# Cross attention with a routed expert layer: the last pair of batches taken out of the loop

## The chip, the cores and the metric

The program runs on one core of one Trainium2 chip. Its time is the device time of one execution in microseconds (us). A core has TensorE (PE in the rows, with its weight loads listed apart as PEld), VectorE (DVE), ScalarE (ACT), GpSimd (POOL) and SyncE (SP), which here only issues DMAs. Each runs its own instruction stream in order, and they meet at semaphores.

## The reference

```python
x = x + xattn(layernorm(x), ctx_768, Wq, Wk, Wv, Wo, bo)
x = x + ffn(layernorm(x), router_weight, router_bias, gate_w, up_w, down_w, shared_*)

# xattn: 16 heads of 64, x (16, 256, 128), context (16, 1601, 96)
sim  = einsum('bhid,bhjd->bhij', q, k) * SCALE
out  = einsum('bhij,bhjd->bhid', softmax(sim), v)   # then @ Wo + bo

# ffn: 32 experts of width 64, four per token, and a shared expert of width 128
scores = sigmoid(tokens @ router_weight.T)          # two of four groups, then the best four
hidden = silu(tokens @ gate_w) * (tokens @ up_w)    # per expert
y      = sum of topk_w * (hidden @ down_w) + shared expert
```

## The kernel before

**Attention.** The 16 batches are taken in pairs by a hardware loop `Fori(0, B // 2)`, whose body holds both batches (`par` 0 and 1). A batch is four groups of four heads (`i` 0 to 3), so there are 64 groups. I number them from 0: the last batch is groups 60 to 63. A group has S = 13 steps over tiles of 128 keys (the last of 65). In a step `t`, PE makes the scores of tile `t` (`scores`, six matmuls of 512 columns: the precision is kept by splitting every operand in a hi and a lo part, hi\*hi + hi\*lo + lo\*hi), and adds tile `t-2` to the output (`weigh`, six more). ACT makes the exponentials twice (`exp`: `p_full`, then the rounded `p_hi`), and the difference `p_lo` is made by DVE, or in steps 3, 5, 7 and 9 by POOL (`POOL_STEPS`). `p_full` has two buffers, so `exp(s)` waits for `p_lo` of `s-2`. At the end of a group PE makes the scores of tiles 0 and 1 of the next group.

**Side jobs.** Between these, PE does small jobs into the two PSUM banks of `side`, in the places that `PLACES` and `EXTRA` give: M (32 per group, the scores by which the next group's maximum is found; DVE reduces each), T (the maxima turned to a row, which a DMA sends into `qT_hi`), Q (two per group, the queries of the group after next), Y (four per group, the output projection of the four heads before, which DVE adds to `x1` in `add_head`), and once per batch L and N (normalised tokens turned, for the next batch and for the expert layer) and R (router logits). `s_fill` counts the jobs made, `s_drain` those used, and PE waits for the job before the last one to be drained. POOL splits the next batch's context into hi and lo, one quarter per group (`piece_hi`, `piece_lo`). The loop is the same for every batch, so the last batch also makes L, Q, M, T, two scores and the split for a batch that does not exist.

**Between the stages.** After the loop PE projects the last four heads (`project_head`), turns the last batch's tokens, makes their logits and turns the first routing weights, each of these behind the DVE work that feeds it (`add_head` four times, `token_stats`, `normalise`, `keep_x2f`). ACT and DVE split the first NA = 5 of the expert weights (`weights_hi`, `weights_lo`) there. The other twelve land by DMA after the loop and are split between the first pairs.

**Expert stage.** Straight code: eight chunks `c` of 512 tokens, in each NP = 17 pairs `q` of experts (pair 0 is the shared one). `g` = 17c + q counts all pairs. For a pair PE makes gate and up (`three` twice, three matmuls each), spreads the routing weights over the rows (`rep`, one matmul, not for pair 0), and projects the hidden values of pair g-3 down (three matmuls). ACT does Silu and `h_hi`, DVE `gu_mul` and `hid`, POOL `h_lo`. PE's gate of pair g waits for Silu of g-2 and its up for `hid` of g-2. `turn_routing(c+1)` stands after pair 10 of chunk c, and `keep_routing` on ACT keeps it in `wT`.

## Time and profile before

| | us |
|---|---|
| three runs | 3332.54, 3332.04, 3326.1 (median 3332.04) |
| the profiled execution | 3330.03 |
| its span in the trace | 3327.9 |
| PE busy | 3285.5 (99%) |
| DVE busy | 2399.7 (72%) |
| ACT busy | 1937.8 (58%) |
| POOL busy | 1062.4 (32%) |

Attention fills the span from about 38 to 2986.7 us, the expert stage that from 2997.6 us to the end. A matmul's row gives a duration that overlaps with the next one's (they are pipelined), so what an instruction costs PE is the distance from its start to the next start. Idle time in front of an instruction, with what ended it, stands in square brackets.

### The profile page before, as it was taken

Reading aid. Unit: us, or ns where it says so; the run is one execution under the profiler, and the core shown is the slowest. Engines: PE = TensorE matmul, PEld = TensorE weight load, DVE = VectorE, ACT = ScalarE, POOL = GpSimd, SP = SyncE. Lnnn points to the kernel's source line nnn. Section 1 sums busy time; section 2 is a strip of 40 time slices with the busy share of each in tenths; the row PEclk is TensorE's granted clock in tenths of the full one; section 3 lists DMA queues with packets and bytes.
Section 4 is the critical chain, followed back from the end, with each engine's and each line's share of the span. In section 5 each row is a group of like instructions: output and inputs, shape, how many; then the busy total and the mean of one; then the engine's idle time right before and its main releaser. Section 6 shows DMA issues by size and latency. Waiting matters only on the chain.

```text
span 3327.9 us, 50432 instructions
## 1 busy us (share of the span) xinstructions
PE 3285.5 (99%) x15589; PEld 2616.2 (79%) x15589; DVE 2399.7 (72%) x4954; ACT 1937.8 (58%) x2239; POOL 1062.4 (32%) x724
## 2 busy tenths in 40 slices
PE   8999999999999999999999999999999999999999
PEld 6777777777787777777777777777777777777887
DVE  6777777777777777777777777777777777777655
ACT  4655556665566555565555565555656566655554
POOL 4322233222332222322223322233222332225555
PEclk9999999999999999999999999999999999999999
DMA  2000000000000000000000000000000000010000
GB/s 91 1 16 1 17 1 16 1 1 17 1 16 1 17 1 16 1 9 10 1 16 1 17 1 16 1 16 2 1 16 1 17 1 16 1 45 4 7 7 10
DMA packets 8682, 35.98 MB, mean 11 GB/s; under 512 B 1657, under 2 KB 2306, under 8 KB 8130
## 3 DMA queue, kind: packets, MB, share of 16 engines
q1 hardware_dynamic: 8386, 32.29, 3.1%
q8 instruction: 154, 2.52, 0.3%
q14 instruction: 142, 1.16, 0.1%
HBM read 29.92 MB, written 2.10 MB: 10 GB/s over the span
## 4 chain that ended last, share of the span: by engine, by line
issue 71%; POOL 18%; PE 9%; DVE 1%; POOLq 0%; ACT 0%; DVEq 0%; ACTq 0%
POOL p_lo L391 12%; POOL cT_lo L380 2%; PE st L629 2%; POOL v_lo L382 2%; PE st L631 2%; PE st L630 2%; POOL cT_hi L372 1%; POOL v_hi L373 1%; PE op L629 1%; PE op L631 1%; PE op L630 1%; PE side L676 1%; POOL rstd L309 1%; DVE gu_mul L1123 0%; POOLq L390 0%
## 5 line engine op out<-in xcount | busy, mean ns | idle before, releaser
L760 ACT ACTIVATE p_full<-st 128x1024 f32<-128x1024 f32 (+1 forms) x832 | 855.9, 1029 | 1158.4 <-PE st L520 1154.1
L1032 DVE TENSOR_REDUCE m_part<-side 128x1 f32<-128x402 f32 x2048 | 1095.0, 571 | 544.0 <-PE side L460 544.0
L391 POOL TENSOR_TENSOR p_lo<-p_full,p_hi 128x1024 fp32r<-128x1024 f32 x256 | 649.9, 2539 | 2087.6 <-ACT p_hi L763 2087.6
L763 ACT ACTIVATE p_hi<-st 128x1024 fp32r<-128x1024 f32 (+1 forms) x832 | 850.9, 1023 | 0.0
L1020 DVE TENSOR_TENSOR p_lo<-p_full,p_hi 128x1024 fp32r<-128x1024 f32 (+1 forms) x576 | 700.5, 1216 | 140.2 <-ACT p_hi L763 116.7
L460 PE MATMUL side<-cT_hi,qT_hi 96*128 96x402 f32 x2048 | 563.0, 346 | 0.0
L514 PE MATMUL st<-qT_hi,cT_hi 97*128 97x512 f32 (+1 forms) x1668 | 539.8, 405 | 2.3 <-DMA qT_hi<-m_row 2.3
L528 PE MATMUL op<-p_hi,v_hi 128*97 128x512 f32 (+1 forms) x1664 | 527.7, 398 | 6.1 <-DVE p_lo L1020 6.1
L517 PE MATMUL st<-qT_lo,cT_hi 96*128 96x512 f32 (+1 forms) x1668 | 528.0, 397 | 0.0
L520 PE MATMUL st<-qT_hi,cT_lo 96*128 96x512 f32 (+1 forms) x1668 | 523.2, 395 | 0.0
L531 PE MATMUL op<-p_lo,v_hi 128*97 128x512 f32 (+1 forms) x1664 | 519.4, 393 | 0.0
L534 PE MATMUL op<-p_hi,v_lo 128*97 128x512 f32 (+1 forms) x1664 | 519.2, 393 | 0.0
L460 PEld LDWEIGHTS side<-cT_hi,qT_hi 96*128 96x128 f32 x2048 | 385.1, 188 | 114.0
L520 PEld LDWEIGHTS st<-qT_hi,cT_lo 96*128 96x128 f32 (+1 forms) x1668 | 307.0, 184 | 83.7
L517 PEld LDWEIGHTS st<-qT_lo,cT_hi 96*128 96x128 f32 (+1 forms) x1668 | 308.9, 185 | 80.9
L531 PEld LDWEIGHTS op<-p_lo,v_hi 128*97 128x97 f32 (+1 forms) x1664 | 269.9, 162 | 115.6
L534 PEld LDWEIGHTS op<-p_hi,v_lo 128*97 128x97 f32 (+1 forms) x1664 | 269.8, 162 | 114.8
L514 PEld LDWEIGHTS st<-qT_hi,cT_hi 97*128 97x128 f32 (+1 forms) x1668 | 297.7, 186 | 31.6 <-issue 2.8
L528 PEld LDWEIGHTS op<-p_hi,v_hi 128*97 128x97 f32 (+1 forms) x1664 | 265.1, 163 | 38.0 <-DVE p_lo L1020 8.4
L414 POOL TENSOR_TENSOR h_lo<-hid,h_hi 128x512 fp32r<-128x512 f32 x136 | 175.8, 1293 | 142.7 <-ACT h_hi L826 142.6
L912 DVE SCALAR_TENSOR_TENSOR x<-side,recip,x 128x128 f32 (+1 forms) x520 | 158.6, 347 | 11.2 <-DVE recip L909 2.6
L1123 DVE TENSOR_TENSOR gu_mul<-st,act_g 128x512 f32<-128x512 f32 x128 | 88.4, 691 | 102.7 <-PE side L676 95.7
(153 smaller groups left out, 2629.5 us busy)
## 6 DMA issues: line engine op xcount, KB each, us to landing
keys_nat<-in_ctx_keys SPq DMA_DIRECT2D x18, 624.0 KB, 5.7
keys_tur<-in_ctx_turned SPq DMA_DIRECT2D x18, 603.0 KB, 4.9
out_x<-x SPq DMA_DIRECT2D x8, 256.0 KB, 2.0
x<-in_x SPq DMA_DIRECT2D x1, 1920.0 KB, 12.2
w_rest<-in_moe_w SPq DMA_DIRECT2D x1, 1152.0 KB, 7.4
qT_hi<-m_row SPq DMA_DIRECT2D x65, 4.0 KB
w_first<-in_moe_w SPq DMA_DIRECT2D x1, 960.0 KB, 4.7
aw<-in_attn_w SPq DMA_DIRECT2D x2, 448.0 KB, 5.3
```

The source lines that it names most:

```text
L391: pool.tensor_tensor(p_lo[:, slot(s), :], p_full[:, s % 2, :], p_hi[:, slot(s), :].bitcast(F32), ALU.subtract).then_inc(s_lo_pool, 1)
L460: return pe.matmul(where[:, 0:MAXW], qT_hi[0:DC, slot, tile * P:(tile + 1) * P], cT_hi[0:DC, par, part * MAXW:(part + 1) * MAXW], start=Tr ...
L514: pe.matmul(st[0:m, s % 2, j, :], cT_hi[:, par, keys], qT_hi[:, slot, halves[j]], start=True, stop=False)
L517: pe.matmul(st[0:m, s % 2, j, :], cT_hi[0:DC, par, keys], qT_lo[:, slot, halves[j]], start=False, stop=False)
L520: mm = pe.matmul(st[0:m, s % 2, j, :], cT_lo[:, par, keys], qT_hi[0:DC, slot, halves[j]], start=False, stop=True)
L528: pe.matmul(op[0:OW, j, :], v_hi[0:m, par, s, :], p_hi[0:m, slot(s), halves[j]], start=(s == 0), stop=False)
L531: pe.matmul(op[0:OW, j, :], v_hi[0:m, par, s, :], p_lo[0:m, slot(s), halves[j]], start=False, stop=False)
L534: mm = pe.matmul(op[0:OW, j, :], v_lo[0:m, par, s, :], p_hi[0:m, slot(s), halves[j]], start=False, stop=(s == S - 1))
L760: act.activation(p_full[0:m, s % 2, :], both(st[0:m, s % 2]), ACT.Exp, scale=SCALE)
L763: act.activation(p_hi[0:m, slot(s), :], both(st[0:m, s % 2]), ACT.Exp, scale=SCALE).then_inc(s_ex, 1)
L1020: dve.tensor_tensor(p_lo[0:m, slot(s), :], p_full[0:m, s % 2, :], p_hi[0:m, slot(s), :].bitcast(F32), ALU.subtract).then_inc(s_lo, 1)
L1032: dve.tensor_reduce(m_part[:, at:at + 1], where[:, 0:MAXW], AX.X, ALU.max).then_inc(s_drain, 1)
```

## The change

1. The loop runs over seven pairs of batches. The eighth pair is written out behind it with constants in place of registers (`turns`, `here`), its second batch with `last` set.
2. With `last`, nothing is made for what does not come: no L and Q in group 62, no M, T and Q in group 63, no scores of a next group, and no context is loaded or split in the last batch.
3. The expert weights land in one tensor `gud_raw` that lies over context and query buffers of batch 14 (each of these tensors is now two, one per half). Three DMAs are issued in group 60 and a small one in group 63. ACT splits weights 0 to 8 in group 62 and 9 to 16 in group 63, one behind an `exp`. DVE makes `gud_lo` in group 63, two behind a step, in place over `gud_raw`. The tokens of chunk 0 are split there too (`x2_hi_of(0)`, `x2_rest(0)`), and `wT` is cleared at the start of the program.
4. The expert stage begins right behind the last `weigh`. `turn_routing(0)` stands behind pair 0. The last batch's four heads are projected behind pairs 1 to 4, its tokens turned behind pair 9, its logits made behind pair 11, all in bank 1 of `op`. ACT changes its table to Exp and back behind pair 12. In every chunk `turn_routing(c+1)` moves from behind pair 10 to behind pair 14, `keep_routing` from 11 to 15.

```diff
-        def jobs_of(par, i):
-            return JOBS0 + par * PER_BATCH + offset[i]
+        def places(i, last=False):
+            drop = {2: "LQ", 3: "MTQ"}.get(i, "") if last else ""
...
+        def turns(eng, body):
+            with eng.Fori(0, B // 2 - 1) as bb:
+                for par in range(2):
+                    for i in range(NGB):
+                        body(bb, par, i, False)
+            for par in range(2):
+                for i in range(NGB):
+                    body(B // 2 - 1, par, i, par == 1)
...
+                if last and i == 0:
+                    sp.wait_ge(s_v, NG)
+                    sp.wait_ge(s_oe, NG - 3)
+                    load_moe_weights(0, 0, 4)
+                    load_moe_weights(1, 4, 10)
+                    load_moe_weights(2, 10, 16)
...
 # PE, end of a group
                 pv(S - 2)
+                if last and i == NGB - 1:
+                    pv(S - 1)
+                    return
...
-            pe.wait_ge(s_oe, NG + 1)
-            for h in range(GH):
-                pe.wait_ge(s_drain, JOBS_END + h - 1)
-                project_head(bank(JOBS_END + h), (NGB - 1) * GH + h, h * NQ)
-            pe.wait_ge(s_drain, JOBS_END + GH - 1)
-            turn_tokens(bank(JOBS_END + GH), B + 2, 2)
-            pe.wait_ge(s_drain, JOBS_END + GH + 1)
-            route_logits(bank(JOBS_END + GH + 1))
...
+            def last_batch_jobs(q):
+                where = op[:, 1, :]
+                if 1 <= q <= GH:
+                    h = q - 1
+                    pe.wait_ge(s_wk, 1)
+                    pe.wait_ge(s_drain, JOBS_END + h)
+                    project_head(where, (NGB - 1) * GH + h, h * NQ)
+                elif q == 9:
+                    pe.wait_ge(s_drain, JOBS_END + GH)
+                    turn_tokens(where, B + 2, 2)
+                elif q == 11:
+                    pe.wait_ge(s_drain, JOBS_END + GH + 1)
+                    route_logits(where)
...
+                    if g == 0:
+                        pe.wait_ge(s_rw, B)
+                        pe.wait_ge(s_oe, NG + 1)
+                        turn_routing(0)
                     if g >= 3:
                         down(g - 3)
+                    if c == 0:
+                        last_batch_jobs(q)
...
-                    if q == 10 and c + 1 < NCH:
+                    if q == 14 and c + 1 < NCH:
...
 # ACT, in a group
                     exp(s)
+                    if last and i == 2 and 1 <= s <= 9:
+                        weights_hi(s - 1)
+                    elif last and i == 3 and 2 <= s <= 9:
+                        weights_hi(s + 7)
+                    elif last and i == 3 and s == 1:
+                        x2_hi_of(0)
...
 # ACT, expert stage
+                    if g == 0:
+                        keep_routing(0)
+                    if g == 10:
+                        act.wait_ge(s_fill, JOBS_END + GH + 1)
+                        keep_x2(op[:, 1, :], slice(B * NQ, (B + 1) * NQ))
+                    if g == 12:
+                        act.preload_act_table(ACT.Exp)
+                        keep_exponentials(op[:, 1, :], JOBS_END + GH + 2)
+                        act.preload_act_table(ACT.Silu)
...
 # DVE, in a group
                     side_jobs(at[t][1])
+                    if last and i == NGB - 1:
+                        for q in (2 * t - 4, 2 * t - 3):
+                            if q < NP:
+                                weights_lo(q)
...
 # DVE, expert stage
+                    if c == 0:
+                        if 1 <= q <= GH:
+                            dve.wait_ge(s_drain, JOBS_END + q - 1)
+                            add_head(op[:, 1, :], JOBS_END + q, NG * GH + q, (T, T + 1))
+                        elif q == 5:
+                            dve.wait_ge(s_drain, JOBS_END + GH)
+                            token_stats((T, T + 1), 2)
+                        elif q == 7:
+                            normalise((T, T + 1), 2, B + 2)
+                        elif q == 10:
+                            keep_x2f(op[:, 1, :], B + 1)
+                        elif q == 13:
+                            exponentials_seen(B + 1)
```

PE before, from the last `weigh` but one of group 63 to the first pair. L514 to L520 are the scores of a group that does not come, L540 the four heads, L427 and L432 tokens and logits, L635 `turn_routing(0)`, L629 to L631 `three`:

```order
L514 MATMUL st<-qT_hi,cT_hi 128x512 x2
L517 MATMUL st<-qT_lo,cT_hi 128x512 x2
L520 MATMUL st<-qT_hi,cT_lo 128x512 x2
L612 REGISTER_ALU
L612 COMPARE_AND_BRANCH
L540 MATMUL side<-B_all,oT 128x129 x8
L427 MATMUL side<-ident,xn 128x128 x2
L432 MATMUL side<-rwT,x2f 128x32 x2
L635 MATMUL op<-ident,w_all 64x128 x4
L629 MATMUL st<-x2_hi,gud_hi 128x512
```

PE now, from the last `weigh` (L549 to L555) through pair 0 (L642 to L644 twice); L648 is `turn_routing(0)`:

```order
L549 MATMUL op<-p_hi,v_hi1 97x512 x2
L552 MATMUL op<-p_lo,v_hi1 97x512 x2
L555 MATMUL op<-p_hi,v_lo1 97x512 x2
L642 MATMUL st<-x2_hi,gud_hi 128x512
L643 MATMUL st<-x2_lo,gud_hi 128x512
L644 MATMUL st<-x2_hi,gud_lo 128x512
L642 MATMUL st<-x2_hi,gud_hi 128x512
L643 MATMUL st<-x2_lo,gud_hi 128x512
L644 MATMUL st<-x2_hi,gud_lo 128x512
L648 MATMUL op<-ident,w_all 64x128 x4
```

The two scores are gone, pair 0 stands directly behind the attention, and the jobs that stood between the stages have moved behind the first pairs.

DVE before, in group 63. L1020 is `p_lo`, L1032 the reduction of one M, L1030 and L1019 the sums for its waits on registers, L909 and L912 `add_head`:

```order
L909 RECIPROCAL recip<-side 128x2
L910 REGISTER_ALU
L912 SCALAR_TENSOR_TENSOR x1<-side,recip,x1 128x128 x2
L1030 REGISTER_ALU
L1032 TENSOR_REDUCE m_part<-side 128x1
L1030 REGISTER_ALU
L1032 TENSOR_REDUCE m_part<-side 128x1
L1019 REGISTER_ALU
L1020 TENSOR_TENSOR p_lo<-p_full,p_hi 128x1024
```

DVE now, in the same steps. L1055 is `p_lo`, L1036 `weights_lo`, L948 the mark that the exponentials of R are seen, L936 and L939 `add_head`:

```order
L1055 TENSOR_TENSOR p_lo<-p_full,p_hi 128x1024
L1036 TENSOR_TENSOR gud_lo<-gud_raw,gud_hi 128x384 x4
L1055 TENSOR_TENSOR p_lo<-p_full,p_hi 128x1024
L948 MEMSET spare 128x1
L1036 TENSOR_TENSOR gud_lo<-gud_raw,gud_hi 128x384 x4
L1055 TENSOR_TENSOR p_lo<-p_full,p_hi 128x1024
L1036 TENSOR_TENSOR gud_lo<-gud_raw,gud_hi 128x384 x2
L936 RECIPROCAL recip<-side 128x2
L939 SCALAR_TENSOR_TENSOR x1<-side,recip,x1 128x128 x2
```

Where the 32 reductions of M stood, 17 splits of weights stand.

## Rows read from the trace of the kernel before

**Rows 1.** The page: busy time, share of the span and instructions by engine.
```profile
PE 3285.5 (99%) x15589; PEld 2616.2 (79%) x15589; DVE 2399.7 (72%) x4954; ACT 1937.8 (58%) x2239; POOL 1062.4 (32%) x724
```

**Rows 2.** Windows at the expert stage: window, its length, busy by engine, granted clock.
```profile
2997.50:3001.50 4.00, 4.00 (x11) 3.19 (x10) 0.69 (x1) 2.32 (x3) 0.00 (x0) 0.50 0.00 0
3001.50:3041.00 39.50, 39.50 (x176) 32.32 (x175) 29.81 (x46) 26.30 (x50) 23.80 (x19) 1.00 0.00 1
```

**Rows 3.** Timeline, PE, group 63 (start, us, engine, line, operation, count).
```profile
2959.72 0.53 PE L460 MATMUL side<-cT_hi,qT_hi 96*128 96x402 f32 x2
2960.08 0.63 PE L528 MATMUL op<-p_hi,v_hi 128*97 128x512 f32 x2
...
2979.69 0.28 PE L453 MATMUL side<-x_hi,A_hi 128*96 128x256 f32 x1
...
2981.11 0.63 PE L528 MATMUL op<-p_hi,v_hi 128*97 128x512 f32 x2
...
2982.50 0.62 PE L514 MATMUL st<-qT_hi,cT_hi 97*128 97x512 f32 x2
...
2983.90 0.62 PE L528 MATMUL op<-p_hi,v_hi 65*97 65x512 f32 x2
...
2986.69 1.06 PE L540 MATMUL side<-B_all,oT 97*128 97x129 f32 x8
```

**Rows 4.** Timeline, PE, from the stage change to the third pair.
```profile
2993.76 0.66 PE L427 MATMUL side<-ident,xn 128*128 128x128 f32 x2 [3.92 <-DVE xn L879]
...
2997.57 0.78 PE L629 MATMUL st<-x_hi,gud_hi 128*128 128x512 f32 x1
...
3002.46 0.40 PE L629 MATMUL st<-x_hi,gud_hi 128*128 128x512 f32 x1
```

**Rows 5.** Page: the exponentials, p_lo on DVE and on POOL (mean ns of one).
```profile
L760 ACT ACTIVATE p_full<-st 128x1024 f32<-128x1024 f32 (+1 forms) x832 | 855.9, 1029 | 1158.4 <-PE st L520 1154.1
L391 POOL TENSOR_TENSOR p_lo<-p_full,p_hi 128x1024 fp32r<-128x1024 f32 x256 | 649.9, 2539 | 2087.6 <-ACT p_hi L763 2087.6
L1020 DVE TENSOR_TENSOR p_lo<-p_full,p_hi 128x1024 fp32r<-128x1024 f32 (+1 forms) x576 | 700.5, 1216 | 140.2 <-ACT p_hi L763 116.7
```

**Rows 6.** Timeline, ACT, around the stage change.
```profile
2985.49 1.03 ACT L745 ACTIVATE oT<-op 97x1024 f32<-97x1024 f32 x1 [3.59 <-PE op L534]
...
2987.43 2.16 ACT L799 ACTIVATE gud_hi<-w_first 128x384 fp32r<-128x384 f32 x5
...
2997.34 1.28 ACT L819 ACT_TABLE_LOAD   x1
2998.64 0.59 ACT L810 ACTIVATE wT<-op 64x512 fp32r<-64x512 f32 x1
2999.23 0.60 ACT L844 ACTIVATE act_g<-st 128x512 f32<-128x512 f32 x1
```

**Rows 7.** Timeline, DVE: two heads added, one pair of experts, one weight split.
```profile
2988.26 0.17 DVE L909 RECIPROCAL recip<-side 128x2 f32<-128x2 f32 x1
...
2989.11 0.17 DVE L909 RECIPROCAL recip<-side 128x2 f32<-128x2 f32 x1
...
3004.34 0.69 DVE L1123 TENSOR_TENSOR gu_mul<-st,act_g 128x512 f32<-128x512 f32 x1 [0.20 <-PE side L676]
...
3005.67 0.93 DVE L1095 TENSOR_TENSOR gud_lo<-w_rest,gud_hi 128x384 fp32r<-128x384 f32 x1
```

**Rows 8.** Timeline, POOL, at that weight split.
```profile
3004.89 1.30 POOL L414 TENSOR_TENSOR h_lo<-hid,h_hi 128x512 fp32r<-128x512 f32 x1 [0.66 <-ACT h_hi L826]
```

**Rows 9.** Timeline, PE, a head projected in a running group.
```profile
2965.19 0.61 PE L540 MATMUL side<-B_all,oT 97*128 97x129 f32 x4
2965.55 0.72 PE L514 MATMUL st<-qT_hi,cT_hi 97*128 97x512 f32 x2
```

**Rows 10.** Waits (us in total, times, longest): PE and DVE where the loop jumps back.
```profile
PE op L528 <- DVE p_lo L1020: 6.1, 7, 1.0
DVE p_lo L1020 <- issue: 23.5, 7, 3.5
```

More of the change, by code:

```diff
@@ L139, in xattn_moe @@
         s_rl = sem("router_landed")
-        s_mw = sem("first_moe_weights_landed")
-        s_mr = [sem(f"other_moe_weights_{part}_landed") for part in range(3)]
+        s_mw = [sem(f"moe_weights_{part}_landed") for part in range(4)]
         s_id = sem("identity_ready")
@@ L407, in x2_rest, with body @@
                                    x2_hi[:, c % 2, :].bitcast(F32), ALU.subtract).then_inc(s_xxl, 1)
-            x2_rest(0)
+            def body(bb, par, i, last):
+                g = group_of(par, i)
+                for s in POOL_STEPS:
+                    pool.wait_ge(s_ex, bb * (2 * NGB * S) + (g * S + s + 1))
+                    pool.tensor_tensor(p_lo[:, slot(s), :], p_full[:, s % 2, :],
+                                       p_hi[:, slot(s), :].bitcast(F32), ALU.subtract).then_inc(s_lo_pool, 1)
+                    if s == 3 and i == 1:
+                        deviations(bb * 2 + (par + 2), slice(0, 4))
+                    elif s == 5 and not last:
+                        piece_hi(bb, par, i)
+                    elif s == 7 and not last:
+                        piece_lo(bb, par, i)
+                    elif s == 7 and i == NGB - 1:
+                        x2_rest(0)
+            turns(pool, body)
             for c in range(NCH):
@@ L459, in max_scores @@
                 tile, part = k % (NM // 4), k // (NM // 4)
-                return pe.matmul(where[:, 0:MAXW], qT_hi[0:DC, slot, tile * P:(tile + 1) * P],
-                                 cT_hi[0:DC, par, part * MAXW:(part + 1) * MAXW], start=True, stop=True)
+                return pe.matmul(where[:, 0:MAXW], qT_hi[slot][0:DC, tile * P:(tile + 1) * P],
+                                 cT_hi[par][0:DC, part * MAXW:(part + 1) * MAXW], start=True, stop=True)
             def turn_maxima(where):
@@ L587, in pv @@
                     weigh(s, par)
-                at = places(i)
+                at = places(i, last)
                 for t in range(2, S):
@@ L810, in keep_routing @@
                 act.activation(wT[0:2 * E, c % 2, :], op[0:2 * E, 1, :], ACT.Copy).then_inc(s_wk, 1)
-            after_attention(act)
-            x2_hi_of(0)
-            for q in range(NA):
-                weights_hi(q)
-            act.wait_ge(s_fill, JOBS_END + GH + 1)
-            keep_x2(bank(JOBS_END + GH), slice(B * NQ, (B + 1) * NQ))
-            keep_exponentials(bank(JOBS_END + GH + 1), JOBS_END + GH + 2)
-            act.preload_act_table(ACT.Silu)
-            keep_routing(0)
             def hidden_hi(g):
@@ L834, in _ @@
                     g = c * NP + q
-                    if c == 0 and NA <= q + 2 < NP:
-                        weights_hi(q + 2)
                     if q == 3 and c:
@@ L1005, in _, with weights_lo, body @@
             head_steps, loop_steps = steps[0], [0]
-            def body(bb, par, i):
-                g = group_of(par, i)
-                n = dve.snap(bb * (2 * NGB * S) + g * S)
-                jobs0 = jobs_of(par, i)
-                jobs = dve.snap(bb * (2 * PER_BATCH) + jobs0)
-                links = dve.snap(bb * links_per_turn)
+            def weights_lo(q):
+                dve.wait_ge(s_wh, q + 1)
+                dve.tensor_tensor(gud_lo[:, q, :, :], gud_raw[:, q, :, :],
+                                  gud_hi[:, q, :, :].bitcast(F32), ALU.subtract).then_inc(s_wl, 1)
+            def body(bb, par, i, last):
+                if par == 0 and i == 0:
+                    steps[0] = head_steps
+                g = group_of(par, i)
+                n = here(dve, bb * (2 * NGB * S) + g * S)
+                first_bank = jobs_of(par, i, last)
+                jobs = here(dve, bb * (2 * PER_BATCH) + first_bank)
+                place = job_at(i, last)
+                links = here(dve, bb * links_per_turn)
                 made = dict.fromkeys(KINDS, 0)
-                into = [dve.snap(bb * 4 + (2 * par + (i + (NGB - 1)) // NGB * 2 + q)) for q in range(2)]
+                into = [here(dve, bb * 4 + (2 * par + (i + (NGB - 1)) // NGB * 2 + q)) for q in range(2)]
                 def lo(s):
@@ L1025, in side_jobs @@
                         k = made[kind]
-                        j = job_at[i][kind][k]
+                        j = place[kind][k]
                         made[kind] += 1
-                        where, filled = bank(jobs0 + j), jobs + (j + 1)
+                        where, filled = bank(first_bank + j), jobs + (j + 1)
                         if kind == "M":
@@ L1064, in after_jobs @@
                         route_scores(links)
-                at = places(i)
+                at = places(i, last)
                 lo(0)
```

247 lines of the change are left out of this document (100 added, 147 removed).

## The prediction

> **What bounds the kernel.** I read the page first: PE is busy for 99% of the span, the next engine for 72% [rows 1]. So what counts is PE's work and the few places where it stands. The waits list them: seven of 0.9 us where the loop jumps back [rows 10], and the stage change, seen in the timeline and the windows. In group 63 PE works without a hole on things that nobody will use [rows 3]. Then it stands for up to 3.92 us behind the chain of DVE and ACT work that feeds its small jobs [rows 4], and when the pairs start, the granted clock is 0.50, the 1.2 GHz level, for 4.0 us [rows 2]. After that it is 1.00 and PE is busy all 39.5 us of the window [rows 2]. All sums are made against the profiled execution, 3330.03 us, 2.1 us more than its span. The three runs of before have their mean at 3330.2 and their median at 3332.04, so I take its time as typical.
>
> **Work that goes.** Two M cost PE 2960.08 - 2959.72 = 0.36 us, so 32 cost 5.8. The two Q of group 63 cost 2981.11 - 2979.69 = 1.42, and group 62's two as much, together 2.84. The two scores cost 2983.90 - 2982.50 = 1.40 each, together 2.80 [all rows 3]. L and T are three small matmuls; by 0.09 each and 0.09 for the slower start behind them (the duration 0.72 against 0.63) I take 0.4 [rows 9, 3]. Sum: 11.8 us, all on PE's path, as PE has no hole there.
>
> **What is late next in group 63.** Without M a step is two sets of six matmuls, 2 x 1.40 = 2.8 us of PE. ACT needs two exponentials of 0.92 to 1.03 [rows 5] and one `weights_hi` of 2.16/5 = 0.43 [rows 6], at most 2.5: it keeps up. POOL's `p_lo` takes 2.54 [rows 5], and from the end of a scores set to its `weigh` PE has four sets, 5.6 us, against 2.0 (exp) + 2.54 + some 0.2 of handing over. DVE's load in the whole group: nine `p_lo` of 1.22 are 11.0 [rows 5], 17 splits of about 0.41 are 7.0, four heads of 2989.11 - 2988.26 = 0.85 are 3.4 [rows 7], 21.4 in about 36 us (PE's 24 sets of 1.40, and 2.3 for the heads and R). The split's 0.41 is read so: the row shows 0.93, but POOL's `h_lo` ran until 3004.89 + 1.30 = 3006.19, 0.52 after the split's start, and 0.93 - 0.52 = 0.41 [rows 7, 8].
> That row also shows that a split does not run beside a POOL operation. The Trainium skill says so in SBUF — State Buffer, "Who interferes with whom": DVE and GpSimd share a port pair under an exclusive lock, and a DVE `tensor_tensor` with both inputs in SBUF contends with GpSimd's reads. It speaks against this change, since the M reductions that ran beside POOL's `p_lo` read PSUM and the 17 splits read SBUF; the trace agrees, with the 0.93.
> So I let each split wait for POOL's `p_lo`. In steps 3 to 10 that moves DVE's next `p_lo` to 1 to 2 us before PE needs it, which costs nothing. At the end the cover is gone: the last scores used to be followed by Q (1.42) and the next scores (1.40). Now it is last scores, two `weigh`, last `weigh`: 2.8 us, against exp 2.0 + `p_lo` 1.22 + 0.1, and the `p_lo` before it stands behind three heads. PE waits for 0.1 + 0.4 = 0.5. Bounds: 0, if DVE's queue is early, and 2.5, if a whole POOL `p_lo` lies in the way once.
>
> **The stage change.** Before, from 2986.69 (the end of the attention) to 3002.46 (gate of pair 2) are 15.8 us [rows 3, 4]. After, I call P the end of the last `weigh`. ACT keeps `oT` from P + 0.2 to P + 1.1, loads the table in 1.30 (2998.64 - 2997.34), makes Silu of pair 0 in 0.55 and `wT` in 0.59 (with the distance 2999.23 - 2998.64), and is through at P + 3.5 [rows 6]. PE meanwhile makes pair 0 (six matmuls at 0.23, from 39.50/176, 1.4 us), `turn_routing(0)` (four small ones, 0.45 as a head), gate and up of pair 1, stands at P + 3.2 until P + 3.6 for `wT`, and is at gate 2 at P + 3.8 without the head of pair 1. So 15.8 becomes 3.8: 12.0 us saved. This includes the half clock's share: the thirteen matmuls of pairs 0 and 1 took 3002.46 - 2997.57 = 4.9 us [rows 4], where thirteen at 0.23 take 3.0, so 1.9 us.
>
> **What comes back between the pairs.** Four heads, each 2965.55 - 2965.19 = 0.36 and 0.09 behind it [rows 9]: 1.8. Tokens (two small matmuls) 0.25, logits (two in the order, four in the trace) 0.45. The second head waits for the first `add_head`: Silu of pair 1 ends at P + 4.1, `gu_mul` and `hid` take 3005.67 - 3004.34 = 1.33 with their gap [rows 7], the head 0.85, which is P + 6.4, where PE arrives at P + 5.8: 0.6 us. From pair 3 DVE needs 1.33 + 0.85 = 2.2 us a pair and PE ten matmuls and a head, 2.3 + 0.45, so no more waits. The splits of twelve weights have left ACT and DVE there; token statistics, `normalise` and `keep_x2f` (about 1 us each) stand one to a pair. Sum: 3.1 us, bounds 2.5 (no wait) and 5 (each of four heads waits 0.6).
> The two table loads behind pair 12 cost ACT 2 x 1.30 + 0.3 = 2.9 us. Silu of pair 13 may start 2.3 us after its gate; it starts 1.8 after it. So nothing on PE, with 0.5 to spare.
>
> **Loop.** Six jumps back for seven. DVE stands 23.5/7 = 3.4 us at each, PE 6.1/7 = 0.9 [rows 10]. Saved 0.9. Behind the last jump PE went on at once: the heads begin where the scores end, 2986.69 [rows 3], so leaving the loop is free. `turn_routing` four pairs later, `wT` cleared on POOL at the start, and weights loaded two groups (about 90 us) ahead: 0, hidden by PE's matmuls, and if that cover went each of the first two would cost under 1 us, the small job that it is, and the third the weights' own split of 0.4 to 0.9 once. The waits that routing of the last batch brings in chunk 1 stay as they are.
>
> **Sum.** -11.8 + 0.5 - 12.0 + 3.1 - 0.9 = -21.1. 3330.0 - 21.1 = **3309 us**.
>
> **Rivals.**
> - **The lock holds DVE in group 63.** For it: the 0.93 [rows 7]. Each of POOL's four `p_lo` would push a DVE `p_lo` past PE's need by about 1 us and the end by 2: 4 to 6 us, so 3314. Against: the group has 36 - 21.4 = 14.6 us of DVE to spare, and four times 2.54 are 10.2. Chance 0.12.
> - **The clock falls again.** PE stands 0.4 and 0.6 us and waits at the end of group 63. For it: the 0.50 behind the old change [rows 2]. Against: 0.9 us at each jump back with the page's clock full. Price as before, 1.9 us, up to 4: 3311 to 3313. Chance 0.08.
> - **A table load costs ACT twice its row.** By rows: 1.3 us more in the seam, and 5.5 in place of 2.9 behind pair 12, which is 2.1 past what is to spare: 3312.4. Against it stands the row, where the next operation begins 1.30 after the load [rows 6]. Chance 0.03. The Trainium skill has this as its price: ScalarE: Activation LUTs, "What ACT_TABLE_LOAD costs", about 1283 ns and a drain of about 1380 ns for every switch. The trace agrees with the first part and shows no second.
> - **Slower: the straight pair is fetched too late.** If each of the eight written-out groups started with the 3.4 us that DVE stands at a jump [rows 10] and nothing hid it, 27 us would be added: 3336. It decides from 2.6 us a group. Against: the expert stage is straight code and PE stands nowhere in 39.5 us [rows 2]. Chance 0.02.
> The forecast has the remaining 0.75; a gain of 1 to 3 us beyond it (steps of group 63 that DVE's old drains slowed) is in its own range, 3304 to 3313.
>
> **Range and chances.** The runs of before span 6.4 us, which I add in part: 3302 to 3317. What a measurement can tell from no change is about 0.2%, 6.7 us. Every case but the last is faster by more than 13 us, so faster 0.95. Same 0.03, for a mix of losses that I have not seen, slower 0.02.
>
> **What would show it.** Group 63 about 36 us long in place of 46 (36 + 5.8 + 1.4 + 2.8), PE's waits in it under 1 us. The first Silu load at P + 1.1, `wT` at P + 3, the first matmul of the pairs at the end of the last `weigh`, clock 1.00 throughout. In chunk 0 one wait of PE, for the first `add_head`. Wrong would be: PE waiting on `p_lo` of steps 4 to 10 in group 63, more than 1 us on `hid` in pairs 13 to 15, or a hole at the starts of groups 56 to 62.

## The result, and the profile after

The changed kernel takes 3308.0 us (median of 3304.41, 3308.09, 3309.41 and 3307.89), the kernel before, run beside it, 3330.0 (3332.54, 3332.04, 3326.1 and 3327.93). The ratio is 0.9933 with an interval of 0.9921 to 0.9945. The forecast was 3309. The profiled execution is the one of 3304.41 us.

The page: span, then busy time, share and instructions of each engine, then two of the costliest groups.
```profile
span 3302.4 us, 49053 instructions
PE 3264.6 (99%) x15518; PEld 2600.2 (79%) x15518; DVE 2383.1 (72%) x4915; ACT 1935.8 (59%) x2236; POOL 1052.0 (32%) x710
L416 POOL TENSOR_TENSOR p_lo<-p_full,p_hi 128x1024 fp32r<-128x1024 f32 x256 | 651.6, 2545 | 2088.7 <-ACT p_hi L805 2088.7
L1055 DVE TENSOR_TENSOR p_lo<-p_full,p_hi 128x1024 fp32r<-128x1024 f32 (+1 forms) x576 | 700.3, 1216 | 141.7 <-ACT p_hi L805 122.2
```
PE loses 20.9 us of busy time against [rows 1], with 71 matmuls fewer. Some 5 to 7 of these lie in the head of the program, which is slower in one execution than in another whatever the kernel (experiments 1 and 12): two executions with the same kind of head differ by 14.3 (3285.5 and 3271.2) or 16.1 (3280.7 and 3264.6). The operations themselves cost what they did [rows 5].

Windows of group 63, of the passage to the pairs, and of the pairs from pair 2 to the end of pair 0 of chunk 1 (length, busy by engine PE to POOL, granted clock, then DMA):
```profile
2934.70:2969.60 34.90, 34.38 (x159) 25.88 (x158) 28.24 (x49) 25.72 (x33) 11.35 (x5) 1.00 0.00 1
2969.60:2975.50 5.90, 5.52 (x28) 4.26 (x28) 2.48 (x8) 4.84 (x7) 1.17 (x1) 1.00 0.00 0
2975.50:3013.10 37.60, 37.28 (x173) 30.35 (x172) 25.27 (x52) 21.45 (x38) 21.37 (x18) 1.00 0.00 1
```
The reader is to see the clock, 1.00 in all three where [rows 2] had 0.50, and that PE misses its busy time by 0.5, 0.4 and 0.3 us. The timeline of PE has these three holes one by one (in brackets: idle time and what ended it):
```profile
2968.18 0.70 PE L549 MATMUL op<-p_hi,v_hi 65*97 65x512 f32 x2 [0.52 <-DVE p_lo L1055]
...
2969.65 0.40 PE L642 MATMUL st<-x_hi,gud_hi 128*128 128x512 f32 x1
...
2973.40 0.47 PE L700 MATMUL side<-wT,sel 128*128 128x512 f32 x1 [0.38 <-ACT wT L840]
2973.71 0.61 PE L561 MATMUL op<-B_all,oT 97*128 97x129 f32 x4
2974.07 0.48 PE L642 MATMUL st<-x_hi,gud_hi 128*128 128x512 f32 x1
...
2976.26 0.68 PE L561 MATMUL op<-B_all,oT 97*128 97x129 f32 x4 [0.32 <-DVE x L939]
```
P of the prediction is 2969.65: the first expert matmul starts where the last `weigh` ends, and the 3.92 us behind `xn` [rows 4] are gone. The forecast had 0.5, 0.4 and 0.6 for the three holes. ACT at the same place, the chain that feeds `wT` [rows 6]:
```profile
2969.85 1.03 ACT L777 ACTIVATE oT<-op 97x1024 f32<-97x1024 f32 x1 [2.97 <-PE op L555]
2970.89 1.28 ACT L834 ACT_TABLE_LOAD   x1
2972.19 0.60 ACT L862 ACTIVATE act_g<-st 128x512 f32<-128x512 f32 x1
2972.68 0.58 ACT L840 ACTIVATE wT<-op 64x512 fp32r<-64x512 f32 x1
```
The waits where the loop jumps back, six jumps for seven [rows 10] (PE's row counts the hole at the end of group 63 as its seventh):
```profile
PE op L549 <- DVE p_lo L1055: 5.1, 7, 1.1
DVE p_lo L1055 <- issue: 19.5, 6, 3.6
```

**Where the time went.** The same instructions in both traces cut the span into stretches. Two of the marks, the last `m_neg` of group 62 and the first gate matmul of pair 1 of chunk 1, in the kernel before and after:
```profile
2930.85 0.27 PE L464 MATMUL side<-ident,m_neg 128*8 128x128 f32 x1
3038.67 0.39 PE L629 MATMUL st<-x_hi,gud_hi 128*128 128x512 f32 x1
```
```profile
2924.74 0.28 PE L485 MATMUL side<-ident,m_neg 128*8 128x128 f32 x1
3013.16 0.39 PE L642 MATMUL st<-x_hi,gud_hi 128*128 128x512 f32 x1
```

| stretch | before | after | difference | forecast |
|---|---|---|---|---|
| head, to the first scores | 37.69 | 34.30 | -3.4 | none |
| first turn, to its last `m_neg` | 362.25 | 362.52 | +0.3 | none |
| six turns of the loop | 2208.79 | 2207.19 | -1.6 | none |
| last turn, to group 62's last `m_neg` | 322.12 | 320.73 | -1.4 | -0.9 |
| to the end of the attention | 55.84 | 44.91 | -10.9 | -11.8 + 0.5 |
| to the gate of pair 1 of chunk 1 | 51.98 | 43.51 | -8.5 | -12.0 + 3.1 |
| the rest | 289.2 | 289.2 | 0 | 0 |
| sum | 3327.9 | 3302.4 | -25.5 | -21.1 |

The head has nothing to do with the change, as experiments 1 and 12 show; without it 22.1 us are left, and the medians differ by 22.0. The forecast's 11.8 is not all in its row: L of group 62 lies in the stretch before. It is the 0.4 us between 321.09 there in experiment 2, which still makes L, and 320.73 here.

### The profile page after: what moved, and what is told of

Its sections match the earlier page's. It is cut to its first block, busy times and chain, and to the rows that moved or that the text cites. A ratio compares the mean times of both kernels' runs of the same rounds, so it can differ in the third digit from the quotient of the medians.

```text
span 3302.4 us, 49053 instructions
## 1 busy us (share of the span) xinstructions
PE 3264.6 (99%) x15518; PEld 2600.2 (79%) x15518; DVE 2383.1 (72%) x4915; ACT 1935.8 (59%) x2236; POOL 1052.0 (32%) x710
## 4 chain that ended last, share of the span: by engine, by line
PE 96%; DVE 2%; issue 1%; ACT 1%; POOL 0%; DMA 0%; POOLq 0%; DVEq 0%; ACTq 0%
PE st L535 12%; PE st L538 12%; PE op L549 11%; PE st L541 11%; PE op L555 11%; PE op L552 11%; PE side L481 11%; PE side L561 3%; PE st L642 2%; PE st L644 2%; PE st L643 2%; PE side L474 1%; PE op L642 1%; PE op L643 1%; PE op L644 1%
## 5 line engine op out<-in xcount | busy, mean ns | idle before, releaser
L1067 DVE TENSOR_REDUCE m_part<-side 128x1 f32<-128x402 f32 x2016 | 1078.3, 571 | 535.8 <-PE side L481 535.8
L1055 DVE TENSOR_TENSOR p_lo<-p_full,p_hi 128x1024 fp32r<-128x1024 f32 (+1 forms) x576 | 700.3, 1216 | 141.7 <-ACT p_hi L805 122.2
L481 PE MATMUL side<-cT_hi,qT_hi 96*128 96x402 f32 x2016 | 555.3, 346 | 0.0
L549 PE MATMUL op<-p_hi,v_hi 128*97 128x512 f32 (+1 forms) x1664 | 527.4, 398 | 5.1 <-DVE p_lo L1055 5.1
L555 PE MATMUL op<-p_hi,v_lo 128*97 128x512 f32 (+1 forms) x1664 | 521.1, 394 | 0.0
L555 PEld LDWEIGHTS op<-p_hi,v_lo 128*97 128x97 f32 (+1 forms) x1664 | 270.4, 162 | 115.4
L549 PEld LDWEIGHTS op<-p_hi,v_hi 128*97 128x97 f32 (+1 forms) x1664 | 265.7, 164 | 38.2 <-DVE p_lo L1055 8.1
L939 DVE SCALAR_TENSOR_TENSOR x<-side,recip,x 128x128 f32 (+1 forms) x512 | 156.1, 347 | 10.8 <-DVE recip L936 2.2
```

Of the source, the lines that this page charges most:

```text
L481: return pe.matmul(where[:, 0:MAXW], qT_hi[slot][0:DC, tile * P:(tile + 1) * P], cT_hi[par][0:DC, part * MAXW:(part + 1) * MAXW], start=Tr ...
L549: pe.matmul(op[0:OW, j, :], v_hi[par][0:m, s, :], p_hi[0:m, slot(s), halves[j]], start=(s == 0), stop=False)
L555: mm = pe.matmul(op[0:OW, j, :], v_lo[par][0:m, s, :], p_hi[0:m, slot(s), halves[j]], start=False, stop=(s == S - 1))
L1055: dve.tensor_tensor(p_lo[0:m, slot(s), :], p_full[0:m, s % 2, :], p_hi[0:m, slot(s), :].bitcast(F32), ALU.subtract).then_inc(s_lo, 1)
L1067: dve.tensor_reduce(m_part[:, at:at + 1], where[:, 0:MAXW], AX.X, ALU.max).then_inc(s_drain, 1)
```

## The experiments

Times are medians; "the changed kernel" is the repeat in the first experiment, 3308.9 us. The medians carry the heads, which move single runs by some microseconds. So for the edits near the passage I give a second measure, from the last `m_neg` of group 62 to the gate of pair 1 of chunk 1. The changed kernel takes 88.42 us there in both its profiles:

| experiment | that stretch | more than 88.42 | difference of the medians |
|---|---|---|---|
| 3, stage change as before | 97.76 | 9.3 | 6.0 |
| 4, the 32 M made again | 101.26 | 12.8 | 10.9 |
| 5, the splits twice | 97.48 | 9.1 | 6.6 |
| 6, four table loads | 92.60 | 4.2 | 3.65 |
| 7, a hole at the change | 94.92 | 6.5 | 5.15 |
| 11, maxima in between | 94.72 | 6.3 | 3.4 |

**1. The changed kernel again**, for the head.

> The changed kernel once more, so that the experiments beside it have it on the same chip. Its profile of the first time was 24.6 us under its before profile at the head included: the first scores began at 34.3 us in place of 37.7, because the granted clock had risen at 13 us in place of 28. Theory A (the place where the clock rises in the head varies from execution to execution, and is no part of the change): the profile of this run can show either place, and the time is 3304 to 3310 accordingly. Theory B (the changed head, with wT cleared on GpSimd and no weight load behind the first context, brings the clock up earlier): the clock rises at 13 us again.

3308.94 us, five runs from 3305.02 to 3309.36. The first scores in this profile, of the execution of 3309.36 us, against those of the first profile:
```profile
38.72 1.19 PE L535 MATMUL st<-qT_hi,cT_hi 97*128 97x512 f32 x2 [2.35 <-DMA qT_hi<-m_row]
```
```profile
34.30 1.19 PE L535 MATMUL st<-qT_hi,cT_hi 97*128 97x512 f32 x2 [3.37 <-DMA qT_hi<-m_row]
```
One and the same kernel has both heads, 4.4 us apart, and its spans differ by 4.9. The difference begins earlier, at the first scores for maxima: four matmuls in 1.71 us in the profile of before, in 1.00 in that of after.
```profile
13.40 1.71 PE L485 MATMUL st<-cT_hi,qT_hi 96*128 96x402 f32 x4 [0.68 <-ACT qT_hi L708]
```
```profile
13.39 1.00 PE L506 MATMUL st<-cT_hi,qT_hi 96*128 96x402 f32 x4 [0.68 <-ACT qT_hi L740]
```
The repeat of the changed kernel has the 1.71 here, as the kernel before had. The matmuls reach their full rate at about 13.5 us in one execution and at 28 to 31 in another (read from the distances of their starts; the clock column of a window shows 1.00 in both there). So theory A holds, and 3.4 of the 25.5 us were chance. It is also a likely reason why the runs of a kernel can lie some 4 us apart (3305.02, and 3308.21 to 3309.36), though with one profile per kernel that is seen for single runs only.

**2. Only the pair written out**, nothing else of the change.
```diff
+        def turns(eng, body):
+            with eng.Fori(0, B // 2 - 1) as bb:
+                for par in range(2):
+                    for i in range(NGB):
+                        body(bb, par, i)
+            for par in range(2):
+                for i in range(NGB):
+                    body(B // 2 - 1, par, i)
...
-            with pe.Fori(0, B // 2) as bb:
-                for par in range(2):
-                    for i in range(NGB):
-                        body(bb, par, i)
+            turns(pe, body)
...
```

> The kernel before with only part 1: the last pair of batches behind the loop with constants, nothing left out, old stage change. My theory: one jump back less, 0.9 us faster, all else the same, 3329. Rival (the straight code is fetched too late): 3.4 us more at each of eight group starts, up to 27 us slower, 3357, and VectorE's waits named issue grow with the groups 56 to 63.

3329.57 against 3330.55 of the kernel before, ratio 0.9995 (0.9986 to 1.0004): no change that the runs can tell. The traces show the jump: the last turn takes 321.09 us, against 322.12 and 322.01 in the two profiles of the kernel before. Its waits:
```profile
DVE p_lo L1028 <- issue: 20.6, 6, 3.6
PE op L540 <- DVE p_lo L1028: 5.8, 6, 1.1
```
Six stops of DVE of 3.4 us in place of seven, and none at the starts of the eight written-out groups: the 27 us of the slower rival are excluded. The six turns take 2209.39 us here, as before, so writing out is not where their 1.6 us went.

**3. The stage change as before**: heads, tokens, logits and routing stand between the attention and the experts again; the rest of the change stays.
```diff
+            pe.wait_ge(s_oe, NG + 1)
+            for h in range(GH):
+                pe.wait_ge(s_drain, JOBS_END + h - 1)
+                project_head(bank(JOBS_END + h), (NGB - 1) * GH + h, h * NQ)
+            pe.wait_ge(s_drain, JOBS_END + GH - 1)
+            turn_tokens(bank(JOBS_END + GH), B + 2, 2)
+            pe.wait_ge(s_drain, JOBS_END + GH + 1)
+            route_logits(bank(JOBS_END + GH + 1))
...
-                    if c == 0:
-                        last_batch_jobs(q)
...
```

> The changed kernel with part 4 undone: the four heads, the tokens and the logits of the last batch stand between attention and pairs again, and the exponentials are made before the one change of table. Parts 1 to 3 stay. My theory: from the end of the last weigh to gate 2 it takes 11.0 us to the first gate and 4.9 at the low clock, 15.9, where the changed kernel takes 4.1 and gives back 2.8 between the pairs: 9 us slower than the changed kernel, about 3317. Rival (the gap was mainly the weight splits that stood in it, which part 3 has moved): then the gap shrinks to under 6 us without a fall of the clock, and the time is within 3 us of the changed kernel.

3314.92 us, from 3314.44 to 3319.17: +6.0 in medians. The medians fell on different sides of the two groups of runs; like with like it is 3314.4 against 3305 and 3319.2 against 3309.4, and the spans with the early head (first scores at 34.43 and 34.30) are 3312.4 and 3302.4: +9.4 to +10. Its timeline of PE, and the window behind it:
```profile
2971.60 1.56 PE L560 MATMUL side<-B_all,oT 97*128 97x129 f32 x8 [1.11 <-ACT oT L781]
...
2978.89 0.66 PE L447 MATMUL side<-ident,xn 128*128 128x128 f32 x2 [3.49 <-DVE xn L906]
```
```profile
2972.00:2983.00 11.00, 6.42 (x27) 5.21 (x27) 5.11 (x22) 1.78 (x3) 0.69 (x1) 0.51 0.00 0
```
The holes and the clock at its lower level are back together. This part is worth the 9 that it was given. It also answers the rival: the twelve weight splits are still out of the pairs here, and from the first expert matmul to the gate of pair 1 of chunk 1 it takes 41.12 us, as the kernel before did (41.10 and 41.44). Moving them gave nothing there by itself.

**4. The 32 M of group 63 made again**, read by nobody.
```diff
-            drop = {2: "LQ", 3: "MTQ"}.get(i, "") if last else ""
+            drop = {2: "LQ", 3: "TQ"}.get(i, "") if last else ""
...
-                        if kind == "M":
+                        if kind == "M" and last and i == NGB - 1:
+                            max_scores(where, k, 1, 1).then_inc(s_fill, 1)
+                        elif kind == "M":
...
-                            if k == NM - 1:
+                            if k == NM - 1 and not (last and i == NGB - 1):
```

> The changed kernel with the 32 scores for maxima of group 63 made and reduced again, from buffers that are still there (their result goes nowhere); T, Q, L and the next scores stay out. My theory: the 5.8 us of TensorE come back whole, and VectorE then has 32 x 0.57 = 18.3 us more in a group of 42 us, 40 us of load with the splits: it becomes the bound, so 6 to 10 us slower than the changed kernel, 3314 to 3318. Rival (TensorE's work there was not on the path, the group ran at VectorE's pace anyway): less than 3 us.

3319.79 us: +10.9, above the 6 to 10 expected, and 12.8 in the stretch itself, where the matmuls alone are 5.8. PE waits for the maxima, and DVE shows why:
```profile
2945.48 0.94 PE L481 MATMUL side<-cT_hi,qT_hi 96*128 96x402 f32 x2 [1.20 <-DVE m_part L1069]
...
2963.43 0.45 PE L481 MATMUL side<-cT_hi,qT_hi 96*128 96x402 f32 x1 [1.86 <-DVE m_part L1069]
```
```profile
2959.55 3.34 DVE L1038 TENSOR_TENSOR gud_lo<-gud_raw,gud_hi 128x384 fp32r<-128x384 f32 x2
2962.81 1.68 DVE L1069 TENSOR_REDUCE m_part<-side 128x1 f32<-128x402 f32 x3
```
Two splits take 3.34 us in place of 1.02, since POOL's `p_lo` runs; the maxima stand behind them and PE behind the maxima, 4.5 us in four holes. The other 2.5 are matmuls that come slower than in full flow, more than half of that in the M behind the holes (two in 0.94 us in place of 0.53). Leaving M out did not only save PE's 5.8 us, it made the room on DVE into which the weights' splits fit.

**5. The splits twice**: 17 more subtractions of 128x384 on DVE in group 63.
```diff
+                hi = gud_hi[:, q, :, :].bitcast(F32)
+                if q:
+                    dve.wait_ge(s_dump, q)
+                dve.tensor_tensor(dump[:, :, :], hi, hi, ALU.subtract).then_inc(s_dump, 1)
                 dve.tensor_tensor(gud_lo[:, q, :, :], gud_raw[:, q, :, :],
...
```

> The changed kernel with one more VectorE subtraction of 128x384 from SBUF in front of each of the 17 weight splits of group 63 (its result is not used). My theory (the lock is real, but lies in VectorE's spare time): 17 x 0.41 = 7 us more of VectorE in a group in which the trace of the changed kernel shows 28.2 us busy of 34.6, so at most one or two waits of TensorE for p_lo: 0 to 2 us slower, 3309 to 3311. Rival (the group stands at the edge, each split behind a GpSimd p_lo pushes the next p_lo out): 4 us or more slower, and TensorE's waits for p_lo grow by that.

3315.51 us, +6.6, and 9.1 in the stretch: my 0 to 2 fell. Nor was it DVE that came late. POOL's timeline, PE's, and the window behind PE's hole:
```profile
2939.87 6.69 POOL L418 TENSOR_TENSOR p_lo<-p_full,p_hi 128x1024 fp32r<-128x1024 f32 x1 [20.27 <-ACT p_hi L807]
```
```profile
2946.62 1.17 PE L551 MATMUL op<-p_hi,v_hi 128*97 128x512 f32 x2 [3.62 <-POOL p_lo L418]
```
```profile
2946.60:2950.00 3.40, 3.38 (x10) 2.57 (x11) 0.00 (x0) 2.35 (x3) 1.33 (x1) 0.50 0.00 0
```
DVE issued subtractions 0.47 us apart with no gap, then its own `p_lo`, until 2944.36; POOL's, released at 2939.87, ended 2.2 us behind that, at 2946.56. So each can shut the other out: a DVE split waits for a running POOL operation (3.34 above), and here POOL's waited for a run of DVE's. But this happened once in four `p_lo`, and not in the changed kernel, which has such runs too. There four splits stand 0.47 apart, POOL's `p_lo` is released in the middle, takes 2.61 us, and the fourth split stands for it (DVE's row, then POOL's):
```profile
2938.92 4.17 DVE L1036 TENSOR_TENSOR gud_lo<-gud_raw,gud_hi 128x384 fp32r<-128x384 f32 x4
```
```profile
2940.06 2.61 POOL L416 TENSOR_TENSOR p_lo<-p_full,p_hi 128x1024 fp32r<-128x1024 f32 x1 [20.29 <-ACT p_hi L805]
```
What decides which of the two goes first is not shown. Of the 9.1 us only 3.8 are idle time of PE; the rest is the lower clock, which lasted from 2945.4 to 2955.7 us.

**6. Two more table loads behind pair 12** (four for two).
```diff
                         act.preload_act_table(ACT.Exp)
+                        act.preload_act_table(ACT.Silu)
+                        act.preload_act_table(ACT.Exp)
                         keep_exponentials(op[:, 1, :], JOBS_END + GH + 2)
```

> The changed kernel with four changes of table behind pair 12 in place of two. In the changed kernel Silu of pair 13 starts at 3003.9, hid of pair 13 ends at 5.9 and TensorE needs it some 1.1 us later. My theory (a load costs its row, 1.30, and the spare time is 1.1): 2.6 more on ScalarE, 1.5 us slower. Rival 1 (each load costs a drain as well, 2.66): the two loads had used up the spare time and the time grows by 5.3. Rival 2 (more spare time behind it, in the second buffer): no change, and TensorE shows no wait at pairs 14 and 15.

3312.59 us, +3.65, and 4.2 in the stretch. ACT and PE:
```profile
3003.92 1.28 ACT L871 ACT_TABLE_LOAD   x1
3005.21 1.28 ACT L872 ACT_TABLE_LOAD   x1
```
```profile
3011.45 0.63 PE L648 MATMUL op<-ident,w_all 128*64 128x128 f32 x4 [2.48 <-DVE spare L950]
```
```profile
3011.40:3014.30 2.90, 2.85 (x11) 2.38 (x12) 1.27 (x2) 1.95 (x4) 1.79 (x3) 0.68 0.00 0
```
The loads stand 1.29 apart: a load costs its row and nothing behind it. But 2.57 us of them gave a hole of 2.48, so only 0.1 was to spare and not the 0.5 of the forecast, and for another reader: not a product of pair 13, but the next `turn_routing`, which waits for DVE's mark that `ex` has been read. The matmuls behind the hole ran partly at the lower clock, which is the 1.7 us that the stretch has beyond the hole.

**7. A hole at the stage change**: four more table loads ahead of the first Silu.
```diff
             act.preload_act_table(ACT.Silu)
+            for _ in range(2):
+                act.preload_act_table(ACT.Exp)
+                act.preload_act_table(ACT.Silu)
```

> The changed kernel with four more changes of table in front of the first Silu, 5.2 us in which TensorE can do pair 0, the routing and gate and up of pair 1, and then stands about 5.5 us for wT. Theory A (a hole of this size has the clock fall as in the old stage change, 0.50 for some 4 us behind it): 5.2 + 1.9 = 7 us slower, 3316. Theory B (it fell there because all of TensorE's work in 11 us was thin, and one hole between full work does not do it): 5.2 us slower, 3314, and the clock is 1.00.

3314.09 us, +5.15.
```profile
2980.95 0.77 PE L700 MATMUL side<-wT,sel 128*128 128x512 f32 x1 [5.55 <-ACT wT L843]
```
```profile
2979.00:2983.00 4.00, 2.05 (x7) 1.89 (x8) 1.83 (x3) 2.79 (x5) 1.12 (x1) 0.50 0.00 0
2983.00:2987.00 4.00, 4.00 (x17) 3.23 (x16) 2.41 (x8) 1.59 (x3) 1.44 (x2) 0.76 0.00 0
```
The hole grew by 5.17 and the clock did fall to 0.50. The median is the one of the theory without it, 5.15, but the stretch that holds the edit took 6.5 us more: 5.17 of hole, some 1.7 of slower matmuls, less the 0.32 that PE no longer waited for the first `add_head`. That is theory A with its 1.9 a little too large. The 1.4 that the median lacks are found in the profile ahead of the edit, where nothing was changed: the first turn took 361.88 us here and 362.5 in both profiles of the changed kernel, the six turns 2206.70 against 2207.19 and 2207.74.

**8 to 10. Two edits for a faster version**, together and apart: the Silu table is loaded before the last `oT` instead of behind it, and DVE's routing of the last batch comes in some fifteen pieces over several chunks instead of five blocks in chunk 1.
```diff
+            act.preload_act_table(ACT.Silu)
             keep_output(NG * S)
-            act.preload_act_table(ACT.Silu)
...
-                    if c == 1:
-                        if q == 5:
-                            route_groups()
...
+                    if 1 <= c <= 4 and q % 2:
+                        next(routing, None)
...
```

> The changed kernel with two changes. The first Silu table is loaded before the last oT is kept, while ScalarE waits for the last weigh (it stood 2.97 us there), so wT comes 1.3 us earlier: TensorE's waits of 0.38 for wT and of 0.32 for the first add_head go. VectorE's routing of the last batch, five blocks of 2.9 to 4 us in chunk 1 behind each of which TensorE stood (0.92, 1.11, 0.75 and 1.28 us), is cut into about 15 pieces, one behind every second pair of chunks 1 and 2. My theory: 0.7 + 4.1 = 4.8 us faster than the changed kernel, 3304. Rival (the pieces meet GpSimd's h_lo more often, each waiting for it): the second part gives less than 2 us.

> The changed kernel with one line moved: the early Silu table load stands before the last copy of the attention output on ScalarE instead of behind it. In the changed kernel PE waits 0.38 us for the copy of the first combine weights (the chain: that copy 1.03, table load 1.28, first activation 0.60, weights 0.58). Theory: the 0.38 us goes, nothing else: 3308.2 against 3308.9 of the changed kernel, which five rounds can hardly tell from no change; the profile must show no wait for wT. Rival: of the 5.8 us of the version with both edits the early load carries more than its wait, since the load now stands in front of the attention output that the last projection needs and the whole order around the stage shifts: then 3306 or below.

> The changed kernel with VectorE's routing of the last batch cut into some fifteen pieces over the chunks 1 to 4 of pair 12, in place of five blocks in chunk 1. In the changed kernel PE waits for the gated product (hid) before the pairs of chunk 1 0.92, 1.11, 0.75 and 1.28 us. Theory: these 4.1 us go and nothing else changes: 3304.8 against 3308.9. The two edits apart then add up to the 5.8 of both, within the measurement. Rival: the delay is only moved to the later chunks, where the pieces stand before VectorE's products in the same way: less than 2 us, 3307 or above, and the trace shows waits on hid in the chunks 2 to 4.

Both: 3303.1 us, ratio to the kernel before 0.9920 (0.9907 to 0.9934), 5.8 under the changed kernel. The load alone: 3308.07; the routing alone: 3303.64, which five runs cannot tell from both. From the first expert matmul to the end of the span the traces have 332.7 us for the changed kernel, 332.1 with the load, 327.6 with the routing and 327.0 with both: -0.6, -5.1, -5.7, which add up. The routing gave 1.0 more than its four waits. In chunk 1 and the first pair of chunk 2 PE had waited four times for `hid`, as it had before the change (0.47, 1.16, 1.21 and 1.31). The first and the last of the four in the repeat of experiment 1, between which stand 1.11 and 0.75:
```profile
3043.43 0.50 PE L642 MATMUL st<-x_hi,gud_hi 128*128 128x512 f32 x1 [0.93 <-DVE hid L1137]
...
3061.72 0.50 PE L642 MATMUL st<-x_hi,gud_hi 128*128 128x512 f32 x1 [1.29 <-DVE hid L1137]
```
With the routing in pieces none of the four is left and none comes in later chunks. With the early load PE's 0.38 for `wT` is gone, but the 0.32 for the first `add_head`, which was to go as well, is still there. Now `oT` starts when its input is there, and no load stands in front of Silu:
```profile
2971.28 1.28 ACT L833 ACT_TABLE_LOAD   x1
2974.25 1.03 ACT L777 ACTIVATE oT<-op 97x1024 f32<-97x1024 f32 x1 [1.69 <-PE op L555]
2975.17 0.59 ACT L862 ACTIVATE act_g<-st 128x512 f32<-128x512 f32 x1
```

**11. Maxima in place of the extra subtractions** of experiment 5: as many DVE operations on the same data, with one input instead of two.
```diff
-                dve.tensor_tensor(dump[:, :, :], hi, hi, ALU.subtract).then_inc(s_dump, 1)
+                dve.tensor_reduce(dump[:, :], hi, AX.X, ALU.max).then_inc(s_dump, 1)
```

> As the kernel with the splits twice, but the seventeen extra operations of VectorE in group 63 are maxima over the same 128x384 (one input) in place of subtractions with two inputs in SBUF; nothing reads them. With the subtractions GpSimd's p_lo took 6.69 us in place of 2.54, PE waited 3.62 us, and the time rose by 6.6. Theory A (what holds GpSimd off is the run of operations with two SBUF inputs): the maxima leave gaps for GpSimd, its p_lo stays under 3.5 us, PE does not wait there, time within 1 us of the changed kernel, 3309 to 3310. Theory B (any run of VectorE operations that reads SBUF holds GpSimd off, or VectorE's load as such is what makes its own p_lo late): p_lo of GpSimd again over 5 us or VectorE's p_lo late, 3312 or above.

3312.32 us, +3.4, and 6.3 in the stretch. POOL's `p_lo` took 2.78, 3.30, 3.70 and 2.53 us, one of them above the 3.5 that A allowed, none near the 6.69. That fits A in the main, but does not prove it, since POOL got in between plain subtractions in the changed kernel too. Here it is DVE that stands (DVE, then PE):
```profile
2961.30 2.24 DVE L1042 TENSOR_TENSOR gud_lo<-gud_raw,gud_hi 128x384 fp32r<-128x384 f32 x1
2963.46 1.21 DVE L1061 TENSOR_TENSOR p_lo<-p_full,p_hi 128x1024 fp32r<-128x1024 f32 x1
```
```profile
2964.73 1.07 PE L551 MATMUL op<-p_hi,v_hi 128*97 128x512 f32 x2 [3.41 <-DVE p_lo L1061]
```
The time is that of B. DVE in this group has room for the 17 splits and not for 17 operations more, of either kind. The clock was 0.50 for 3.4 us behind the hole, which with holes of 4.1 us more than in the changed kernel makes the 6.3.

**12. The kernel before again**, for its head.

> The kernel before once more, for the profile of its head. Its first profile and that of the changed kernel differ by 25.6 us where the medians differ by 22; 3.4 us of that lie ahead of the first scores (37.69 against 34.30). Theory A: the place in the head at which the granted clock rises differs between executions of one kernel, so first scores lie anywhere from 34 to 39 us here too, and the time from the first scores to the end is 3292.3 to 0.5 us each time. Theory B: the head of the kernel before is always the slow one: first scores at 37.7 again, and the changed kernel's other late heads (38.0 to 38.7) are something else.

3327.71 us in the one run; first scores at 34.58, span 3325.6. The kernel before has both heads as well, so theory A again. From the first scores to the end it takes 3290.2 and 3291.0 us in its two profiles (the last above the 0.5 that I allowed), the changed kernel 3268.1 and 3268.6: 21.6 to 22.9 us for the change, with the head taken out.

## Why the prediction was right

- **Work that goes, 11.8, less the new wait of 0.5: 11.3.** Measured 10.9, or 11.3 with the 0.4 of L that lies in the stretch before. The wait at the end of group 63 is 0.52, for the reason given: the last `p_lo` without Q and the next scores as its cover. The three heads in front of it, part of the forecast's reason, did not matter: DVE stood 0.93 us for the exponential before it. Only M was tried by itself (experiment 4); Q and the two scores were not.
- **Group 63.** The forecast took 10.0 us from it (46 to 36); from the first scores that lost an M to P it is 44.6 us before (2942.14 to 2986.69) and 35.0 after (2934.68 to 2969.65), 9.6 less. DVE was busy 28.2 us and not 21.4: the splits did stand behind POOL's `p_lo`, as the weighing of the lock said, and it cost nothing with M gone. A split by itself is 0.47 us from start to start, where the forecast had 0.41. Beside the four in 4.17 us (experiment 5):
```profile
2957.00 3.70 DVE L1036 TENSOR_TENSOR gud_lo<-gud_raw,gud_hi 128x384 fp32r<-128x384 f32 x3
```
  The rival's mechanism was there and found cover. Experiments 4, 5 and 11 show where the cover ends: with 32 M or 17 operations more it costs 6 to 9 us beyond the work that PE itself gets.
- **The stage change, 12.0, and what comes back, 3.1: 8.9.** Measured 8.5, and 9.3 to 10 when that part alone is undone. Gate 2 stands at P + 4.4 with a head of 0.36 in it, 4.1 against the 3.8 forecast. The wait for the first `add_head` is 0.32 and not 0.6: PE came to it at P + 6.3 and not 5.8, and the head was added at P + 6.6 and not 6.4. No other head waits.
- **The clock.** 1.00 throughout, so the rival fell in this kernel; experiments 5, 6, 7 and 11 show that it lay a few microseconds of idle PE away.
- **The table loads.** The load costs its row (1.28, and 1.29 to the next in a run of five), so that rival fell. "With 0.5 to spare" was wrong: it was 0.1, and a reader that I had not followed came first.
- **The loop, 0.9.** One jump less is 0.9 to 1.0 (experiment 2). The stretches ahead of group 63 lost 2.7 in all. The 1.6 in the six turns had no term: they take 2208.8, 2209.0 and 2209.4 us in three traces without the rest of the change, and between 2206.3 and 2208.1 (mean 2207.2) in the eleven with it. Some 0.7 of it is PE's wait for `p_lo` behind the six jumps, 5.5 us in all without it and 4.8 with it, on average. What in the change does that, and the rest, stays open.
- **The sum**, 21.1, stands against 22.1 in the traces without the head. The large terms came out by the mechanisms that the forecast named. That the total is only 1 us off is in part luck: two small errors ran against each other. With L counted where it lies, the forecast took 0.4 too much from the passage and 1.4 too little from what is ahead of it.

## What to carry to other kernels

A job that makes what nobody reads costs more than its matmuls: price also the engine that drains it (in experiment 4, 5.8 us of matmuls cost 12.8), and who gets that engine's room. Small dependent chains between two stages, which cost holes and the clock behind them, belong between independent blocks of the next stage, in pieces as small as the slack of one block; and when you write "x to spare", follow every reader of what comes later, not only the nearest. Before you explain a difference of two profiles, lay both into the same stretches: an eighth of this one was a head that varies by itself. The same holds for medians: the stretch that holds the edit told experiment 7's two theories apart, and the median did not.

## What the runs showed of the hardware

- The head's matmuls reach their full rate at about 13.5 or at 28 to 31 us, from one execution of the same kernel to the next. The first scores move by 4.4 us with it in the changed kernel and by 3.1 in the kernel before, the end by 4.9 and 2.3.
- In experiment 5 a run of DVE subtractions with two inputs in SBUF kept a POOL subtraction waiting for as long as it lasted (6.69 us in place of 2.5). In the changed kernel POOL got into such a run (2.61), and the DVE subtraction behind it took 2.76 us in place of 0.55. With a one-input maximum between each two, POOL's took 2.5 to 3.7, and DVE's next subtraction up to 1.7 us more.
- Behind a hole of 1.86 us on PE (experiment 4) the window shows the clock at 1.00; with holes of 2.48, 3.41, 3.62 and 5.55 us it was at 0.50 for 3 to 10 us. The hole alone does not decide: in experiment 3 it was 0.50 from 2972.3 on, behind a wait of 1.11 us and small matmuls, before the hole of 3.49. Nor does the fall stand at one place: in experiments 5 and 7 it came inside the hole, in experiment 6 some 1 us behind it, where the first matmuls of 512 columns still stand 0.24 apart and those after 3012.75 us 0.42.
- Table loads follow each other at 1.28 to 1.29 us, and the next activation starts 1.29 to 1.30 after the last of them.
